# Four fused transformer sublayers on one Trainium2 core: norm scales spread through diagonal tiles, layer-0 values computed beside the projection, routing turned three steps later, layer-1 projection reordered by batch, last experts' first splits moved ahead

## What is computed

```
x = layernorm(x + attention0(x))   # 16 heads of 8; exp(-gamma_h * dist(q,k) / sqrt(8)), only keys after the query's row
x = layernorm(x + moe0(x))         # 64 experts of 88, top 8 of the best 4 of 8 groups, times 2.5; two shared experts of 88
x = layernorm(x + attention1(x))   # k, v from a latent of 32; softmax of scores times exp(-0.01 |i-j|)
x = layernorm(x + moe1(x))         # 8 experts of 512 with gelu, top 2, biases; a shared expert
layernorm(x) = (x - mean(x)) / sqrt(var(x) + 1e-5)
```

## Time and profile before

| quantity | value |
|---|---|
| median of the runs | 1330.66 us (1328.98 to 1332.03) |
| profiled execution, own time | 1337.09 us |
| its span | 1335.2 us |
| mean granted TensorE clock | 0.969 |
| PE, DVE, ACT, POOL busy | 95%, 81%, 68%, 32% of the span |
| DMA traffic | 135.80 MB |

### The profile page before, as it was taken

How to read it: one execution, slowest core, us unless ns; L and a number is a source line. 1 busy time by engine, 2 the same in 40 slices (tenths; PEclk the granted TensorE clock), 3 DMA queues, 4 the chain that set the end, 5 groups by cost and what they waited for, 6 DMA issues and landing times. The chain is left out here.

```text
span 1335.2 us, 21183 instructions
## 1 busy us (share of the span) xinstructions
PE 1271.2 (95%) x7366; PEld 717.4 (54%) x7366; DVE 1088.0 (81%) x1754; ACT 914.5 (68%) x1546; POOL 425.2 (32%) x913
## 2 busy tenths in 40 slices
PE   5999998899999999999999999999999999999998
PEld 1322227678787878787322322332232266777777
DVE  5588874779999999997687889888888547788886
ACT  4899984356665656564527888888888847677774
POOL 4477773102121222120532532452253222213110
PEclk8899998999999999998998999999999988999998
DMA  5423200177766777663265554334332010121200
GB/s 151 128 65 82 81 8 27 51 160 168 154 162 156 160 161 168 151 150 121 79 152 105 151 142 130 99 87 120 96 98 50 22 34 32 66 95 48 95 32 32
DMA packets 69956, 135.80 MB, mean 102 GB/s; under 512 B 13000, under 2 KB 44297, under 8 KB 63049
## 3 DMA queue, kind: packets, MB, share of 16 engines
q1 hardware_dynamic: 68696, 133.40, 39.7%
q10 hardware_dynamic: 1152, 1.05, 0.2%
HBM read 116.93 MB, written 16.29 MB: 100 GB/s over the span
## 5 line engine op out<-in xcount | busy, mean ns | idle before, releaser
L1778 ACT ACTIVATE a_PR<-n1a_C 128x512 f32<-128x512 f32 x576 | 299.5, 602 | 83.0 <-PE n1a_C L1684 82.8
L1793 DVE CUSTOM_DVE_ANT_0 OC_last<-a_mring,a_COR 128x1024 bf16<-128x1024 f32 x256 | 302.9, 1219 | 45.8 <-PE a_mring L1651 45.3
L1621 POOL TENSOR_SCALAR_AFFINE_SELECT a_PR<-a_PR 128x128 f32<-128x128 f32 x512 | 136.2, 296 | 253.9 <-ACT a_PR L1778 253.4
L981 ACT ACTIVATE e_HH<-e_T 128x512 fp32r<-128x512 f32 x176 | 110.9, 633 | 126.1 <-DVE e_T L1021 123.4
L1684 PE MATMUL n1a_C<-a_QP,a_KP 74*128 74x512 bf16 (+3 forms) x768 | 177.0, 333 | 4.7 <-ACT a_PR L1778 3.5
L893 POOL TENSOR_TENSOR e_HL<-e_T,e_HH 128x512 fp32r<-128x512 f32 x43 | 69.6, 1619 | 292.8 <-ACT e_HH L981 292.8
L1703 PE MATMUL n1a_C<-a_PR,a_V 128*9 128x512 f32 (+3 forms) x1536 | 152.2, 492 | 0.0
L459 DVE TENSOR_SCALAR a_PR<-a_PR,a_lo,a_hi 128x1024 f32<-128x1024 f32 (+1 forms) x160 | 118.5, 764 | 36.4 <-ACT a_PR L433 36.2
L1684 PEld LDWEIGHTS n1a_C<-a_QP,a_KP 74*128 74x128 bf16 x768 | 56.9, 98 | 160.0 <-ACT a_PR L1778 120.0
L2094 DVE TENSOR_TENSOR e_HL<-e_GL,e_HH 128x512 fp32r<-128x512 f32 x144 | 109.5, 764 | 38.1 <-ACT e_HH L2057 34.4
L1013 DVE TENSOR_TENSOR e_T<-e_SG,e_psU 128x512 f32<-128x512 f32 x184 | 125.2, 681 | 15.0 <-PE e_psU L908 13.9
(11 more groups left out here) (285 smaller groups left out, 2314.4 us busy)
## 6 DMA issues: line engine op xcount, KB each, us to landing
e_ROUTE<-routing SPq DMA_DIRECT2D x24, 704.0 KB
a_QP<-q_parts SPq DMA_DIRECT2D x72, 192.0 KB
e_RAW<-in_w_chunks SPq DMA_DIRECT2D x46, 192.0 KB, 3.7
a_QM<-q_parts SPq DMA_DIRECT2D x64, 128.0 KB, 2.9
e_GATE<-gates SPq DMA_DIRECT2D x8, 1024.0 KB, 4.6
e_ROUTE<-routing SPq DMA_DIRECT2D x8, 640.0 KB
a_KP<-k_parts SPq DMA_DIRECT2D x24, 192.0 KB
e_ROUTE<-routing SPq DMA_DIRECT2D x8, 576.0 KB
```

Of the source, the lines that this page charges most:

```text
L981: nc.scalar.activation(HH[n % NH][:], T[n % NTR][:], ACT.Copy).then_inc(high_done, 1)
L1621: last = nc.gpsimd.affine_select(out=d, in_=d, compare_op=keep, fill=0.0, base=0, pattern=[[step, P]], channel_multiplier=-step)
L1778: nc.scalar.activation(PR[:, g % NPR, j, :], ring[n % NRING][:], ACT.Exp).then_inc(s_read, 1)
L1793: nc.vector.tensor_tensor_reduce(out=junk[:, i % 2, :], in0=mring[k % 2][:], in1=COR[:, c:c + S], scale=1.0, scalar=-3.0e38, op0=ALU.mult, ...
```

## The change

Five edits, all in the written-out order and two in what is computed where:

1. **Layer 0.** Values and centred X are made in `project_l0`, into two more banks (psV); values of groups 0 and 1 after the norms of group 1, the rest after the other work. The stores of q and k count on different semaphores, and the first pack loads are three of q (after q's stores), then three of k. `attention_l0` no longer does either. The block's semaphores are given back without another barrier (`PassingSems`).
2. **Norms.** DVE builds, per group, a 128x512 tile of four diagonal blocks 128 x inv (`diagonal`), and PE spreads it with one matmul of 512 columns instead of four of 128. The order on PE is variance 0, 1, 2, spread 0, variance 3, spreads 1, 2, 3.
3. **MoE of layer 0.** TURN goes from 20 to 23; three products take their places in the end of the routing chain; the order of the banks that are turned into and their waits follow. Each group's stores have a semaphore, and the first routed chunk's rows are loaded group by group (8 small loads) as these land.
4. **Layer-1 projection.** All engines take batch 0 first; q's halves of both groups before k's. q's packs are loaded once q's eight stores have landed, k's after k's. POOL's thirds start after the fifth remainder. Fill matmuls: 4 and 3 where 5, 6 and 4 stood.
5. **Layer-1 experts.** `AheadMoeL1`: logits, XH, XL and the split of expert 0 run in the block of norm n1a, per group after its rescale (the split on POOL as soon as the weights are loaded), and the experts' banks are those of that norm.

```
 class Norm:
+    def diagonal(self, dve, g):
+        dve.wait_ge(self.inv, self.base + g + 1)
+        blocks = self.Q[g][:].rearrange("p (t c) -> p t c", c=P)
+        self.nc.vector.scalar_tensor_tensor(blocks, self.consts["ident"][:].unsqueeze(1).to_broadcast([P, GW // P, P]), float(P),
+                                            self.inv_of[:, g].unsqueeze(2).to_broadcast([P, GW // P, P]), ALU.mult, ALU.mult)\
+            .then_inc(self.diagonals, 1)
     def spread_inverse(self, pe, g):
-        pe.wait_ge(self.inv, self.base + g + 1)
-        for t in range(GW // P):
-            last = self.nc.tensor.matmul(...)
+        pe.wait_ge(self.diagonals, self.base + g + 1)
+        self.nc.tensor.matmul(self.S[g][:], self.consts["mean_of"][:].to_broadcast([P, P]), self.Q[g][:], start=True, stop=True)\
+            .then_inc(self.spread, 1)
+    def diagonals_and_scales(self, dve):
+        for g in range(NG - 1):
+            self.invert(dve, g)
+            self.diagonal(dve, g)
+        self.rescale(dve, 0)
+        self.invert(dve, NG - 1)
+        self.diagonal(dve, NG - 1)
+        for g in range(1, NG):
+            self.rescale(dve, g)
 class SharedL0:
     def load(self, sp, it):
+        if q == 0:
+            sp.wait_ge(self.q_stored[b], self.Q_STORES)
         for r in range(NPART):
             rows = slice(r, PAIRS, NPART)
             sp.dma_start(self.QP[s][rows], ...).then_inc(got, 16)
+        if q == 0:
+            sp.wait_ge(self.stored[b], self.STORES)
+        for r in range(NPART):
+            rows = slice(r, PAIRS, NPART)
             sp.dma_start(self.KP[s][rows], ...).then_inc(got, 16)
 def moe_l0
-    TURN = 20
+    TURN = 23
-        banks = (psG[0], psU[0], psG[1], psU[1])
+        banks = (psG[1], psU[1], psG[0], psU[0])
-                sp.wait_ge(stored, 16 * NG)
-                for c in range(CHS, CHS + NR):
+                for g in range(NG):
+                    sp.wait_ge(stored[g], 16)
+                    for e, p0, p1 in segments(CHS):
+                        sp.dma_start(ROUTE[CHS % NR][p0:p1, grp(g)], routing[e, grp(g)].partition_broadcast(p1 - p0))\
+                            .then_inc(first_rows[g], 16)
+                for c in range(CHS + 1, CHS + NR):
                     load_route(c)
                 def turn_weights():
                     pe.wait_ge(weights_ready, 1)
-                    pe.wait_ge(silu_done, TURN)
-                    pe.wait_ge(mul_done, TURN)
                     for g in range(NG):
+                        if g % 2 == 0:
+                            pe.wait_ge(silu_done, TURN - 1 + g // 2)
+                            pe.wait_ge(mul_done, TURN - 1 + g // 2)
 def project_l1
+    THIRDS_FROM = 5
+        ORDER = [(2 * b + g, 2 * m + w) for b in range(B) for m in range(2) for g in range(2) for w in range(2)]
+        FIRST = ORDER[0:2 * NV]
-                sp.wait_ge(first_stored, 2 * NV * 2 * 16)
+                sp.wait_ge(first_stored[0], 2 * NV * 16)
                 for g in range(2):
-                    mp.load_first(sp, g)
+                    mp.load_q_group(sp, 0, g, mp.first_loaded[g])
+                sp.wait_ge(first_stored[1], 2 * NV * 16)
+                for g in range(2):
+                    mp.load_k_group(sp, 0, g, mp.first_loaded[g])
+                for n, (g, w) in enumerate(FIRST):
+                    if n == 0:
+                        pool.wait_ge(rest_done, THIRDS_FROM)
 class AheadMoeL1
+    def on_tensor(self, pe, norm, C):
+        pe.wait_ge(self.route_loaded, 32)
+        for g in range(NG):
+            norm.await_done(pe, g)
+            for t in range(TG0):
+                m = g * TG0 + t
+                last = self.nc.tensor.matmul(C[0][:, m * NE1:(m + 1) * NE1], self.X[:, m * P:(m + 1) * P], self.W[:], start=True, stop=True)
+            last.then_inc(self.logits, 1)
```

More of the change, by code:

```diff
@@ L470, in norm_signals @@
 def norm_signals(sem):
-    return {n: sem(f"norm_{n}") for n in ("centred", "squared", "variance", "kept", "dev", "inv", "spread", "done")}
+    return {n: sem(f"norm_{n}") for n in ("centred", "squared", "variance", "kept", "dev", "inv", "diagonal", "spread", "done")}
 class Norm:
@@ L480, in __init__ @@
         self.Q, self.CS, self.dev_of, self.inv_of, self.C, self.S = Q, CS, dev_of, inv_of, C, S
-        self.centred, self.squared, self.variances, self.kept, self.dev, self.inv, self.spread, self.done = (
-            signals[n] for n in ("centred", "squared", "variance", "kept", "dev", "inv", "spread", "done"))
+        self.centred, self.squared, self.variances, self.kept, self.dev, self.inv, self.diagonals, self.spread, self.done = (
+            signals[n] for n in ("centred", "squared", "variance", "kept", "dev", "inv", "diagonal", "spread", "done"))
     def of_x(self, g):
@@ L615, in _ @@
                         norm.keep_with_input(dve, g)
-                for g in range(NG):
-                    norm.invert(dve, g)
-                for g in range(NG):
-                    norm.rescale(dve, g)
+                norm.diagonals_and_scales(dve)
+                if ahead is not None:
+                    ahead.on_vector(dve)
                 norm.finish(dve)
@@ L819, in route_count @@
     def route_count(c):
-        return 16 * sum(len(list(segments(d))) for d in range(CHS, c + 1) if d % NR == c % NR)
+        return 16 * sum(len(list(segments(d))) for d in range(CHS + 1, c + 1) if d % NR == c % NR)
     def on_pool(n):
@@ L962, in _ @@
                     norm.centre(pe, g, Y)
-                for g in range(NG):
-                    norm.variance(pe, g)
-                for g in range(NG):
-                    norm.spread_inverse(pe, g)
+                norm.variances_and_spreads(pe)
             @block.scalar
@@ new lines, in remainder @@
+                def remainder(g, w):
+                    dve.wait_ge(part1, count(g, w))
+                    if g >= 2:
+                        dve.wait_ge(part3, count(g - 2, w))
+                    nc.vector.tensor_tensor(rest[:, w, g % 2], val[:, w, g % 2], part(g, w, 0), ALU.subtract).then_inc(rest_done, 1)
+                dve.wait_ge(dec_loaded, 16)
+                value(0, 0)
+                value(0, 1)
+                remainder(0, 0)
+                remainder(0, 1)
+                value(1, 0)
@@ new lines, in _ @@
+                value(1, 1)
+                value(0, 2)
+                remainder(1, 0)
+                value(0, 3)
+                remainder(1, 1)
+                remainder(0, 2)
+                value(1, 2)
+                remainder(0, 3)
+                value(1, 3)
+                remainder(1, 2)
+                remainder(1, 3)
+                for m in range(2):
+                    for g in (2, 3):
+                        for w in range(2):
+                            value(g, 2 * m + w)
@@ L1895, in experts_l1 @@
+def experts_l1(nc, X, Y, ahead, C, consts, gates_dram, w_experts, signals, out):
     SE = NG * CH1
@@ L2020, in turn @@
                     last.then_inc(turned, 1)
-                pe.wait_ge(route_loaded, 32)
-                for m in range(NT_TOK):
-                    last = nc.tensor.matmul(psR[:, m * NE1:(m + 1) * NE1], X[:, m * P:(m + 1) * P], W[:], start=True, stop=True)
-                last.then_inc(logits, 1)
                 for n in range(N):
```

430 lines of the change are left out of this document (246 added, 184 removed).

## The result

Seven executions of the changed kernel have a median of 1323.05 us (1315.68 to 1326.53), seven of the kernel before 1329.55 (1327.74 to 1333.92); the ratio is 0.9929, with a 95% interval of 0.9909 to 0.9950. So it is faster, by 0.7% or some 9 us (the means are 8.7 us apart, the medians 6.5); I had forecast 1.5% and 1311, and 1323 lies above the range of 1302 to 1319. The profiled execution took 1326.53, its span 1324.6, and its mean granted clock is 0.971 (before: 1337.09, 1335.2, 0.969).

A forecast was written before the change was run, and what follows sets the result against it. Long stages were taken as bound by ACT, PE and DVE and held fixed, with savings at the seams: -6.5 + 0 - 5.0 - 5.5 - 2.6 = -19.6; 1337.09 - 19.6 = 1317.5, less 6.43, gives 1311 us, range 1302 to 1319.

The forecast's parts named there:

- every step at its worst: Whole kernel: the slow ends of all the steps' bounds taken together, 1337.09 - 7 - 6.43 = 1324 us.
- Layer 0, forecast -6.5: Seam before layer 0's attention: first Exp at 33.9 or 37.8 us instead of 42.21, gain 8.3 or 4.4, taken as 6.5.
- The change leaves these stages alone: Layer 0's attention, its MoE and layer 1's experts: these long stages were held fixed, with savings only at seams between blocks.
- The rivals: Those on the clock: it stays up in the norms (1303 us, chance 0.14); half clock in layer 0's seam (1316, 0.08).
- Norms, forecast 0: Four norms: wide spreads cost the same as narrow ones at either clock, diagonals hide under variances; bounds +1 to -2.6 each.
- the rival of cheap wide matmuls: Norms' spreads: 512 columns cost 1.6 times 128 columns, not four times; 15 us less, 1296 us, chance 0.03.
- The turn, forecast -5.0: Layer 0's MoE: 3.9 us from filling PE's hole before the turn, 1.1 from earlier routing rows; bounds -7 and -2.
- second chunk up to 3 late: Layer 0's MoE: routing rows of the second chunk arrive up to 3 us late, leaving that step a gain of 2.
- Projection, forecast -5.5: Layer 1's projection: SP's chain of stores and loads ends earlier, first tile at 664.9 us instead of 670.47.
- the bound of -3: Layer 1's projection: smallest gain, if eight DVE instructions are stretched by 0.8 us at the block's end, less what overlaps.
- Experts, forecast -2.6: Seam before layer 1's experts: first up product at about 1100.7 us instead of 1103.30; bounds -2 and -3.
- The base: Whole kernel: sum made from the profiled execution's 1337.09 us, with 6.43 taken off for its distance above the runs' median.

The follow-up runs named there:

- place: All SBUF tiles of layer 1's experts put back in the old kernel's order, PSUM banks unchanged, against the changed kernel; 1316.35 us, ratio 0.9901 to the kernel before.

## Why the prediction was wrong

The direction held, and so did the seams' mechanisms; the size did not. The step that failed is the assumption under the whole sum, "time saved at a seam is time saved at the end", with the stages behind held fixed. Three of them moved: layer 0's attention from 151.5 to 155.0 in the mean of three traces, the MoE behind its first weighing by 1.5, and the experts' step from 1.362 to 1.387 us. Undone or made alone, the five parts give at equal clock: layer 0 -4.5, turn -3.6, projection -4.2, norms +0.9, experts +1.0, together -10.4, where -19.6 was forecast, and 1332.5 against 1321.8 is -10.7. Each of these is good to 1 or 2 us, so the close agreement is partly luck, and the projection's term is there at equal clock only: its median shows none. That 1323 lies inside the 1324 that I had worked out with every step at its worst is luck too, since not those bounds but other terms came true.

1. **Layer 0, forecast -6.5.** The first Exp came 6.9 earlier in the mean of three traces, and the seam was worked out rightly. What failed is "The change leaves these stages alone": the stage behind took 155.0 in the mean and not 151.5, 1.5 for each fall of the clock in it. The rivals had the clock's cost only at the seams. That the new start brings the falls is not shown: some traces with it have none, and there are only two of the kernel before.
2. **Norms, forecast 0.** Right at equal clock, by the windows above, and the +0.9 can't be told from 0. But the forecast took the fall of the clock inside the norm as given, and it is not: over all traces the stretch takes 7.2 to 13.8 us by where the clock falls, 7.3 to 12.3 of them in the old form. Beside POOL's split of weights the diagonals of n1a took up to 1.01 us and not 0.69 (least, median and most, in ns):

```profile
L567 DVE SCALAR_TENSOR_TENSOR e_T<-ident,r_top x4: 691/692/693, 620.5 to 623.9; 128x512 f32<-128x512 f32 x4
L567 DVE SCALAR_TENSOR_TENSOR n1a_Q<-ident,n1a_inv_of x4: 691/891/1011, 1078.4 to 1082.2; 128x512 f32<-128x512 f32 x4
```

   That agrees with the rule of the Trainium skill ("SBUF — State Buffer", "Who interferes with whom") that a DVE instruction with two inputs in SBUF contends with one of GpSimd (POOL) that reads SBUF. But nothing of it reached the end: the stretch of n1a takes 8.86, that of the MoE's norm without POOL 8.87, both at clock 0.81. Of the rival of cheap wide matmuls nothing is seen: in the experts' stage of the kernel before the median distance from one 512-column matmul to the next is 0.227 us, the least 0.224. The Trainium skill's 131 ns for a sustained matmul of 512 columns ("TensorE: Matmul & The Clock Gate", "Back-to-back issue gap") is not reached here.
3. **The turn, forecast -5.0.** To the first weighing -6.7, more than I summed; behind it 1.5 were given back, net -5.2 in the traces, -3.6 by the version without it at equal clock. The clock, low from 262.1 to 268.9 in the kernel before, does not fall at the turn in any of the three traces of the changed one. Of the loss behind, 0.3 stands in the trace of the changed kernel as a wait for routing rows, the "second chunk up to 3 late" of my bounds, and 0.7 as PE waiting for split weights, which my sum did not have (both in 268 to 310); the rest I did not trace. Other versions with the same turn (the two with the old norms, the one with the two small tiles moved and the one with the doubled scores, 342.6 to 342.7) did not have it, so it depends on the moment.
4. **Projection, forecast -5.5.** -3.6 in the traces, inside the bound of -3; by the medians, without it, nothing. SP's end was right within a microsecond (K's packs are issued by 653.13, 24.1 after the block's start, forecast 23.4). The mis-sized term is the block's other work: the first tile came 29.0 to 30.4 behind the block's start and not 28.2. Its last piece is PE's five filling matmuls, 2.31 us, at half clock (0.50 in the window below, with DVE done at 657.5); at full clock they are half of it, an estimate, and the block would end with DVE, 0.9 earlier.

```profile
656.00:658.40 2.40, 2.40 (x6) 0.58 (x5) 1.52 (x3) 0.55 (x2) 0.00 (x0) 0.50 0.00 0
```

5. **Experts, forecast -2.6.** At the seam -3.7, better than forecast. "The stage is PE-bound from there, so all 2.6 carry" failed, at equal clock the largest miss of the five: PE-bound it is, and just for that reason a step that is 0.025 us longer showed. 144 of them would make 3.6, and the stage is 1.6 longer in the mean (219.8 for 218.2), 1.8 against `place`. The change had moved the tiles, and I had put a move of memory at nothing without a reason. The stage's 1.6 and the seam's 3.7 leave a gain of 2 that the +1.0 does not show; this difference stays open.
6. **The base.** I took 6.43 off for the distance between profiled execution and median of three. The seams' savings were read in an execution with a clock of 0.969, where others of the same kernel had 0.973 on average; whether they are smaller at a higher clock is not shown. At equal clock the kernel before takes 1332.5, so the base of 1330.66 was some 2 us low and the rest of the miss, 9 us, is in the parts. The changed kernel's executions have about the same mean clock (0.973, 0.972, 0.976) as the kernel's before (0.970 to 0.974 in five sets). Against the profiled execution alone the forecast was 1317.5, and the traced executions of the changed kernel took 1326.5, 1319.1 and 1327.3; the medians of its three sets are 1317.6 to 1323.1.

What stays open: what makes an execution have the falls in layer 0's attention. Thin steps are ahead of each, the same thin steps pass without one in other executions, and neither an earlier nor a later start settled it; the distance from the first Exp to the clock's first fall goes with them in 13 of 14 traces. Open too is whether the projection's part gains anything at the end.

## What to carry to other kernels

Time saved at a seam is safe only if the stage behind runs with its clock and its memory layout unchanged; compare the length of every untouched stage, not only the touched ones. When a change moves the allocation of tiles in a PE-bound stage, look at the distance from matmul to matmul: a few nanoseconds on each show in the length of the stage, and the order of allocation is a free thing to repair. Before a sum is made on one profiled execution, set its mean granted clock against that of the timed ones, for here 0.004 of it went with 4 us.

## What I had not expected of the hardware

- The order in which SBUF tiles are allocated, with equal instructions and PSUM banks, moved a group of six 512-column matmuls from 1.362 to 1.387 or 1.397 us.
- The clock fell at the same distance of 20.5 us in each trace with falls, once per pass in the first two to four passes (in the first trace behind 2.00 us in which PE was busy 1.20); the stage takes 1.5 us longer for each.
- The stretch of variances and spreads of the last norm took 7.2 to 10.6 us by the clock it met, in both forms.
- Time and mean granted clock of an execution go together at 0.93 us per 0.001 (kernel before, 91 executions) and 1.12 (changed kernel, 25).
